# A three-layer graph network on one core: the extras and a quarter of the older round's products move ahead of turning the carried columns on TensorE

## What is computed

```
h = x @ W;  a_src = (h * att_src).sum(-1);  a_dst = (h * att_dst).sum(-1)
alpha = leaky_relu(a_src[src] + a_dst[dst])
e = exp(alpha - segment_max(alpha, dst)[dst])
out = segment_sum(e / segment_sum(e, dst)[dst] * h[src], dst)
```

## Time and profile before

| | us |
|---|---|
| median of 3 runs | 6760.7 |
| lowest and highest run | 6745.49, 6763.31 |
| the profiled execution's own time | 6753.64 |
| its span in the trace | 6751.8 |
| TensorE busy | 4889.6 (72%) |
| VectorE busy | 5043.8 (75%) |
| ScalarE busy | 2499.9 (37%) |
| GpSimd busy | 4853.2 (72%) |
| mean granted TensorE clock | 0.763 of full speed |

### The profile page before, as it was taken

One profiled execution on the slowest core, in us unless ns is written; L12 is line 12 of the kernel. 1 busy time (PEld: TensorE's weight loads), 2 busy tenths in 40 slices (PEclk: granted clock), 3 DMA queues, 4 the chain that ended last, 5 costly groups with the idle time before them and its releaser, 6 DMA issues. The chain is left out here.

```text
span 6751.8 us, 104146 instructions
## 1 busy us (share of the span) xinstructions
PE 4889.6 (72%) x21580; PEld 3649.8 (54%) x21581; DVE 5043.8 (75%) x15127; ACT 2499.9 (37%) x4364; POOL 4853.2 (72%) x5234
## 2 busy tenths in 40 slices
PE   6777777777776677777777777595777777777776
PEld 4555555555554555555555555474555555555553
DVE  5777777777777777777777777686777777777778
ACT  3333333333332633333333333393333333333335
POOL 2777777777774577777777777596777777777764
PEclk8777777777777877777777777797777777777777
DMA  8444444444443644454544544374555555555544
GB/s 273 141 140 143 140 140 144 140 140 144 140 141 95 176 144 143 141 145 141 145 141 141 145 141 145 102 232 144 145 149 145 147 148 145 149 145 145 149 132 153
DMA packets 476056, 995.73 MB, mean 147 GB/s; under 512 B 143982, under 2 KB 283556, under 8 KB 475522
## 3 DMA queue, kind: packets, MB, share of 16 engines
q0 software_dynamic: 226928, 635.50, 34.3%
q1 hardware_dynamic: 192448, 305.57, 14.2%
q10 hardware_dynamic: 56402, 51.96, 2.3%
HBM read 921.41 MB, written 71.22 MB: 147 GB/s over the span
## 5 line engine op out<-in xcount | busy, mean ns | idle before, releaser
L1212 POOL DMA_INDIRECT e_rows<-table,e_loaded x4704 | 4488.4, 954 | 1524.4 <-issue 1378.5
L1294 PE MATMUL e_p_mm<-e_rows,e_onehot 128*128 128x264 f32 x9408 | 2421.5, 414 | 0.0
L1294 PEld LDWEIGHTS e_p_mm<-e_rows,e_onehot 128*128 128x128 f32 x9408 | 1880.9, 206 | 348.8 <-issue 0.2
L1414 DVE TENSOR_TENSOR e_rows<-e_rows,e_p_e 128x1024 f32<-128x1024 f32 x1176 | 1418.7, 1206 | 0.0
L1406 DVE TENSOR_TENSOR e_onehot<-e_col,e_p_iota 128x512 f32<-128x512 f32 (+1 forms) x1470 | 951.0, 647 | 295.9 <-issue 293.9
L1503 DVE TENSOR_TENSOR_SCAN e_fwd<-e_mask,e_p_one 64x128 f32<-64x128 bf16 (+1 forms) x294 | 122.0, 415 | 1150.0 <-PE e_p_one L1344 1148.4
L1287 PE MATMUL e_p_mm<-e_xmsg,e_onehot 128*128 128x264 f32 x1764 | 875.4, 668 | 32.9 <-ACT e_p_mm L1242 17.7
L1270 ACT ACTIVATE e_rows<-e_gap 128x64 f32<-128x64 f32 (+1 forms) x294 | 80.5, 274 | 1969.9 <-DVE e_gap L1572 1969.9
L1301 PE MATMUL e_p_one<-ad_parts,e_onehotT 128*128 x5586 | 681.0, 192 | 119.8 <-issue 118.5
L1352 PE MATMUL e_p_small<-ident,e_fwd 64*1 64x64 f32 (+1 forms) x294 | 86.9, 295 | 864.3 <-issue 853.1
L1301 PEld LDWEIGHTS e_p_one<-ad_parts,e_onehotT 128*128 128x128 bf16 x5586 | 552.4, 106 | 291.5 <-issue 185.4
(11 more groups left out here) (238 smaller groups left out, 5626.5 us busy)
## 6 DMA issues: line engine op xcount, KB each, us to landing
e_onehotT<-rel_rows SPq DMA_DIRECT2D x294, 608.0 KB
e_rows<-table,e_loaded POOLq DMA_INDIRECT x4704
n_looprow<-table SPq DMA_DIRECT2D x196, 128.0 KB, 2.6
table<-n_row ACTq DMA_DIRECT2D x98, 132.0 KB, 1.9
table<-n_rows_out SPq DMA_DIRECT2D x14, 910.0 KB, 10.3
table<-n_row ACTq DMA_DIRECT2D x98, 130.0 KB, 3.0
n_inputs<-in_x_turned SPq DMA_DIRECT2D x14, 896.0 KB, 11.0
e_mask<-mask_rows SPq DMA_DIRECT2D x196, 64.0 KB
```

Of the source, the lines that this page charges most:

```text
L1212: pool.indirect_dma_start(rows[k][:, g, 0:TW], None, table[L], bass.IndirectOffsetOnAxis(ap=idx[k][:, g:g + 1], axis=0)).then_inc(s_gat[k] ...
L1294: ins = nc.tensor.matmul(p_mm[:, bass.ds(region, MW)], onehot[:, g, :], rows[k][:, g, :], start=False, stop=True, skip_group_check=True)
L1414: return nc.vector.tensor_tensor(feats, feats, p_e[:, g4, :].unsqueeze(3).to_broadcast([P, 4, H, C]), ALU.mult)
```

## The change

In TensorE's body two calls move up, ahead of the wait for `carry` and the two transposes that raise `colsum`: the products of the extras, which stood right behind these transposes, and the first quarter of the older window's products, which stood behind the transpose that raises `topT`. No instruction is added or taken away, and no other engine's body is changed. In the first round of a phase neither call does anything.

```diff
                     last.then_inc(st["lookup"], 1)
+                    if not first:
+                        extras(past)
+                    products(0)
                     wait_apart(pe, st["carry"], now)
                     for o, src in ((256, outf), (257, outb)):
                         last = nc.tensor.transpose(p_small[0:HG, o:o + 1], flat(src), ident[0:1, 0:1])
                     last.then_inc(st["colsum"], 1)
-                    if not first:
-                        extras(past)
                     wait_apart(pe, st["top"], now)
                     nc.tensor.transpose(p_top[:, 0:HG], top[:], ident[0:HG, 0:HG]).then_inc(st["topT"], 1)
-                    products(0)
                     products(1)
                     products(2)
```

## The result

The changed kernel takes 7352.6 us (median of 4 runs, 7352.3 to 7359.3) against 6762.0 us for the kernel before in the same comparison (median of 4 runs), 1.0879 times as long (95% interval 1.0865 to 1.0894). I had forecast 7510 us, in 7120 to 7660 us: the direction and the range hold, the size was 757 us and came out at 591 us. The profiled execution has a span of 7351.0 us, 599.2 us more than before.

What follows compares the result with a forecast made beforehand. GpSimd's gathers set the pace at about 20.1 us a round; a loop through the loads would take 22.4, 22.9 and 22.9 us, adding 7.8 x 97 = 757 us to 6753.6 us: 7510 us, range 7120 to 7660 us.

Steps and rivals of the forecast that it cites:

- Step 1: From settled to loads landed: 5.2 us in the first phase, 5.7 us in the second and third.
- Step 2: ScalarE's Square, Relu and clearing behind the load: 5.6 us.
- step 3: TensorE's matmuls of the extras, at the 1.2 GHz level: 2.9 us.
- steps 5 to 8: Two transposes 0.3 us, top 0.7 us, quarter 2 to quarter 3's one-hot matrix 3.8 us, hand-overs 0.2 us.
- Step 4: Quarter 0's eight matmuls on TensorE, nearly all slow: 3.7 us, with 1.9 us as the low end.
- TensorE's own round: From one source transpose to the next on TensorE: 21.2 us, under the loop through the loads.
- The fast quarter: Rival: same loop but quarter 0 runs fast, 6990 us, or 7250 us if in half the rounds; 10%.
- It all fits: Rival: the delay is absorbed in VectorE's 4.88 us of idle time, GpSimd keeps the pace, 6754 us; 5%.
- faster: Rival: older products end earlier and release gathers, 6700 us at the very best; 3%.
- the clock never comes back: Rival: TensorE becomes the bound, quarters 1 and 2 take 7.7 us, its round 26.5 us, 8610 us; 2%.

Runs made afterwards that it cites:

- both cuts of the loop: Changed kernel with its loads issued a round earlier, or with ScalarE's clearing moved ahead of Square and Relu of the next window: 6846.7 and 6846.1 us.
- early loads: Loads a round earlier (SyncE waits for fdist, not settled): changed kernel 6846.7 us; kernel before, on the slow chip, 9456.0 us (0.9995).
- the twelve products: Twelve 128x128 products behind the source transpose: changed kernel 7314.9 us, kernel before 6750.7 us, changed kernel with loads a round earlier 6888.9 us.

## Why the prediction was right, and where its size was off

- **The gathers set the pace before, and a loop took it over.** Right. Gaps appeared between gathers, and both cuts of the loop restore 506 of 606 us.
- **Which loop.** Right: load, Square, Relu, clearing, extras, quarter, columns, `top`, quarter 2, one-hot matrix of quarter 3, load. Its hand-overs to ScalarE, TensorE and VectorE show as waits in the trace after, and cutting it at either of two places takes most of the loss away.
- **Step 1, loads.** Too small. I had 5.2 and 5.7 us from `settled` to ScalarE. The mean over 87 rounds is 5.6 us from the issue in the first phase and 5.9 us in the third; with the 0.23 us from `settled` to the issue that is 5.8 and 6.2 us, 0.6 and 0.5 us over my terms. The end of the dense traffic in rows 5 isn't yet the moment at which the reader starts; the round of rows 6, in which ScalarE really waited, was the better row, and I took it as an upper end.
- **Step 2** measured 5.61 us, **step 3** 2.8 us, steps 5 to 8 from the transposes to the next issue 0.27 + 4.70 us in the first phase, 0.27 + 4.96 us in the third (the few tenths for eight heads that I left out are 0.26 us).
- **Step 4, the quarter.** This is the term that was mis-sized: 3.7 us in the sum, 2.8 us measured as the mean in all three phases, between one value of 3.5 and one of 2.5 us in the two rounds shown. My sign for this step was 0.50 as granted clock while the quarter runs; its mean is 0.71. My reason, that the pause ahead of the extras keeps the clock low, doesn't hold as I gave it. The pause is there, longer than I said (1.9 us in the first phase, not 1.2), but with early loads it is 0.1 us and the quarter takes 2.7 to 3.0 us all the same. With the quarter alone moved, a pause of the same length (1.9 us) stands right ahead of the quarter and it takes the full 3.9 us, at a clock of 0.51. There no matmuls stand between the pause and the quarter, in the changed kernel nearly 3 us of extras do. What decides the moment at which the clock comes back, these runs don't show.
- **The sum.** 5.56 + 5.61 + 0.29 + 2.77 + 2.77 + 0.27 + 4.70 = 21.97 us in the first phase, where I had 22.4: 0.9 too much for the quarter, 0.6 too little for the load, the rest small. The mean round there is 22.0 us. Over 97 rounds of three phases the forecast was 7.8 us for the three together, the stretches give 590.8 / 97 = 6.1 us. The load, put too low, made up for part of the quarter, put too high; that much of the nearness of 7510 to 7353 us is luck.
- **TensorE's own round.** Put at 21.2 us with a slow quarter, shown at 20.48 us once the loop is cut. Over three phases it is 1.05 us a round above the gathers' pace, which is the last 100 us of both cut kernels; that it is one value in all phases I hadn't foreseen.
- **The rivals.** The fast quarter was half true: the quarter runs neither slow nor fast as a rule. The Trainium skill, page "TensorE: Matmul & The Clock Gate", section "HAM oscillation — how this bites in real kernels", has waits between bursts let the clock fall. The trace agrees for the long idle stretch of each round, 3 us while TensorE reads words: the mean granted clock during the extras is 0.50 in all three phases. It doesn't bear this out for the pause of 1.9 us just ahead of the extras: they are at 0.50 with it, with 0.3 us between lookups and extras in the first phase of the kernel before, and with 0.1 us with early loads. "It all fits" and "faster" are out, and so is "the clock never comes back": quarters 1 and 2 have a mean clock of 1.00. The Trainium skill's page "Perfetto Trace Analysis", section "Identifying the Most-Contended Engine", ranks engines by occupancy, to say which to optimize first. Here no engine's busy time rose by more than 2% and the time rose by 8.8%, so my reading of the page in this rival, that the time stays where no occupancy rises, is wrong by the measurement.

## What to carry to other kernels

When a piece of work is moved ahead of a hand-over, follow what the piece itself waits for: a wait that ended nowhere before (the clearing behind the loads) becomes part of a loop as soon as its follower stands ahead of the hand-over. Add one turn of that loop from the rows of one round and compare it with the present round; a turn with 1 us of room costs nothing for the first microsecond and everything beyond, so effects of single parts don't add up. Where the new order is wanted all the same, cut the loop at its cheapest place, here one semaphore name or two lines moved, and look for the next loop right below it: here it left the new order 1.5% slower than the old.

## What I had not expected of the hardware

On one chip this program is 1.40 times slower (9462 against 6747 us) without any change. Times in which engines wait for nothing that the profile shows are longer there. The most visible place is the stretch between the source transpose and the first column, in which TensorE reads words into registers; it idled 2.88 us in the round of rows 4. From the run with early loads in the kernel before, on that chip:

```profile
2009.19 0.26 PE L1352 MATMUL e_p_small<-ident,e_fwd 64*1 64x64 f32 x1 [11.23 <-issue]
```

That round is near the long end: over 87 rounds of each phase the idle time there is 5.4 to 6.1 us in the mean (2.1 to 13.4), against 2.9 us on a normal chip. So it makes up 3 of the 9 us by which a round is longer. Ahead of and between the lookups TensorE idles 2.2 to 2.5 us where it idled 0.4, and the pause between two gathers is 0.9 us in the mean where it was 0.3. Single operations have the durations that they have elsewhere: a matmul of the extras 669 against 668 ns, the weighted rows on VectorE 1206 ns on both, ScalarE's Square 2320 against 2318 ns. What slows that chip I didn't settle. Two quarters ahead of the columns make it 2.7% faster there than the kernel before, while they cost 16% on a normal chip: which order is best depends on the chip. Why it turns round there is not shown.

The second surprise is the twelve products: filling a pause of 3 us with work at full clock raised the mean granted clock from 0.809 to 0.870 and yet left the extras of the changed kernel at the low level, since the drop only came later. A mean clock over the whole span says little of the clock where it matters.

The third is the round of 20.48 us that both cut kernels share in all three phases, with a quarter that takes up the difference: a loop that TensorE is part of can settle at a length that none of its pieces sets by itself.
